# Three-tap convolutions on one Trainium2 core: six products per pair of tiles rewritten as five, with the even and odd positions kept apart

## The reference, cut to what matters

```python
CONVS = [(128, 10, 5)] + [(128, 3, 2)] * 4 + [(128, 2, 2)] * 2   # channels, taps, stride
h = x[:, None, :]
for w, g, b, s in zip(conv_ws, ln_gs, ln_bs, strides):
    h = _conv1d(h, w, s)                       # (64, 128, positions)
    h = jnp.swapaxes(h, -2, -1)
    h = _fp32_layernorm(h, g, b)               # over the 128 channels
    h = jnp.swapaxes(h, -2, -1)
    h = jax.nn.gelu(h, approximate=False)
```

## Time and profile before

| | us |
|---|---|
| median of three runs | 940.12 (937.58 to 946.72) |
| the profiled execution, its own time | 938.5 |
| its span, first to last instruction | 936.8 |
| of it: before the convolutions start | 54.9 |
| convolutions | about 490 |
| attention and experts | about 392 |

### The profile page before, as it was taken

How to read it: one execution, slowest core, us unless ns; L and a number is a source line. 1 busy time by engine, 2 the same in 40 slices (tenths; PEclk the granted TensorE clock), 3 DMA queues, 4 the chain that set the end, 5 groups by cost and what they waited for, 6 DMA issues and landing times. The chain is left out here.

```text
span 936.8 us, 12529 instructions
## 1 busy us (share of the span) xinstructions
PE 781.2 (83%) x4371; PEld 585.0 (62%) x4371; DVE 603.2 (64%) x1445; ACT 306.8 (33%) x506; POOL 215.7 (23%) x253
## 2 busy tenths in 40 slices
PE   0059998899979998899989758876888888799987
PEld 0026564556546565466655457866888887689977
DVE  4918655785648746324554556899788889654377
ACT  0043434433442334423422211402223331146433
POOL 3000000000000000000000003655688769148301
PEclk9999998899969899799989669989899999999999
DMA  1350330016000240000000034000000000200000
GB/s 57 44 128 1 63 81 1 0 23 121 1 1 0 33 98 0 0 1 1 1 1 1 0 129 184 1 1 1 1 0 0 0 0 0 75 2 1 1 0 26
DMA packets 22556, 25.34 MB, mean 27 GB/s; under 512 B 17052, under 2 KB 21212, under 8 KB 21404
## 3 DMA queue, kind: packets, MB, share of 16 engines
q1 hardware_dynamic: 22508, 24.74, 10.8%
HBM read 21.05 MB, written 3.66 MB: 26 GB/s over the span
## 5 line engine op out<-in xcount | busy, mean ns | idle before, releaser
L564 PE MATMUL ps<-h,w 128*128 128x400 f32 x720 | 290.9, 548 | 1.8 <-ACT h L632 1.7
L564 PEld LDWEIGHTS ps<-h,w 128*128 128x128 f32 x720 | 139.5, 200 | 106.0 <-issue 103.1
L724 DVE COPY h<-ps 128x800 f32<-128x800 f32 (+2 forms) x58 | 56.6, 975 | 94.4 <-PE ps L564 93.6
L577 PEld LDWEIGHTS ps<-averager,sq 128*100 128x100 f32 (+2 forms) x1024 | 99.3, 171 | 23.0 <-ACT sq L625 19.3
L577 PE MATMUL ps<-averager,sq 128*100 128x1 f32 (+2 forms) x1024 | 99.7, 227 | 8.9 <-ACT sq L625 8.4
L625 ACT ACTIVATE sq<-h 128x800 f32<-128x800 f32 (+2 forms) x58 | 49.8, 858 | 174.2 <-DVE h L724 174.2
L1075 PE MATMUL pt<-for_pe,ident 128*128 128x156 f32 (+2 forms) x420 | 69.9, 328 | 26.5 <-DVE for_pe L1274 26.5
L632 ACT ACTIVATE h<-h,lnp 128x800 f32<-128x800 f32 (+2 forms) x58 | 60.5, 1042 | 86.1 <-DVE h L755 84.4
L755 DVE TENSOR_TENSOR h<-h,ps 128x400 f32<-128x400 f32 (+2 forms) x116 | 60.0, 559 | 39.0 <-PE ps L593 38.9
L604 ACT ACTIVATE h<-ps,lnp 128x800 f32<-128x800 f32 x64 | 63.4, 1011 | 64.0 <-PE ps L525 63.8
L1112 POOL MEMSET eye<- 128x169 f32 x1 | 0.2, 240 | 360.7 <-PE pt L860 360.7
(11 more groups left out here) (272 smaller groups left out, 1156.7 us busy)
## 6 DMA issues: line engine op xcount, KB each, us to landing
late<-windows_dram SPq DMA_DIRECT2D x24, 375.0 KB, 7.5
gate_w<-in_gate_w SPq DMA_DIRECT2D x1, 3456.0 KB, 12.0
up_w<-in_up_w SPq DMA_DIRECT2D x1, 3456.0 KB, 18.7
windows_dram<-parts SPq DMA_DIRECT2D x12, 250.0 KB, 5.2
acts<-in_down_w SPq DMA_DIRECT2D x1, 1728.0 KB, 8.0
w<-in_w SPq DMA_DIRECT2D x1, 1024.0 KB, 5.3
xs<-in_x SPq DMA_DIRECT2D x4, 252.5 KB, 4.2
out_tokens<-hidden SPq DMA_DIRECT2D x6, 96.0 KB, 1.6
```

The costliest lines, as they stand in the source:

```text
L564: mm = pe.matmul(out, w[:, L.first_tap + t, :], source(l, s, 2 * p + c, t), start=(t == 0), stop=(t == L.taps - 1))
L577: mm = pe.matmul(var_ps[0:L.w, at:at + 1], sq[:, n["var"] % 2, c, q * L.w:(q + 1) * L.w], averager[:, 0:1], start=True, stop=True)
L724: nc.vector.tensor_copy(joined(l, s, p, r).rearrange("p (c b) t -> p c b t", c=2), ypair[n["bank"]][:, :, 0:L.cols].rearrange("p c (b t) - ...
```

## The change

Layers 1 to 3 keep their activations as two planes, even and odd positions. Two neighbouring outputs of one signal, at 2j and 2j+1, read the inputs e[2j], o[2j], e[2j+1] and e[2j+1], o[2j+1], e[2j+2] (e even plane, o odd plane). Their first and last taps share e[2j+1]. With w0, w1, w2 the taps, S = (w0+w2)·e[2j+1] is made once, and the outputs are w1·o[2j] + w0·(e[2j]-e[2j+1]) + S and w1·o[2j+1] - w2·(e[2j+1]-e[2j+2]) + S. The two banks of a pair now hold the even and the odd outputs of both chunks' signals, so a "chunk" is a plane.

- PE: "half" is two w1 matmuls and one of S into a bank of its own (`shared_ps`); "conv" is two matmuls of differences. Both wait for the inputs of the whole pair, `inputs_of`.
- GpSimd makes the differences e[i]-e[i+1] of a pair, two operations of 400 columns, into a ring of two (`diff`), as soon as the inputs are there and the pair two before is done.
- ScalarE copies S from PSUM to SBUF (`shared`), at the place of "half" in its queue.
- VectorE's copy out of PSUM becomes an addition of `shared`; w0+w2 and -w2 are made once at the start.
- The sums of squares and the turned rows now share one PSUM bank, so PE's "var" waits for DVE's copy of the rows before (`rows_ready`).
- GpSimd's copy into phases becomes a step at the head of the plan.
- PE's layer-0 matmuls read the windows at a step of two.

```diff
+PAIRED = (1, 2, 3)
+RING = 2
+    if not last:
+        step("phases", 0, 0)()
     prep(0, 2)
     conv(1, 0, 0, first(9))
...
+        shared_ps = ps[:, 6, :]
+        var_ps = ps[:, 7, 256:512]
+        rows_ps = ps[:, 7, 0:256].bitcast(BF16)
+        h0 = sb("h0", [P, 2, GROUP, 2, ROW0 // 2])
...
+        def plane(l, slot, p, parity, cut):
+            n = 2 * LAYERS[l].per_chunk
+            return (h0, h1, h2)[l - 1][:, slot, n * p:n * p + n, parity, cut]
+        def diffs(l, at, cut):
+            return diff[:, at, :].rearrange("p (b t) -> p b t", t=LAYERS[l].pos)[:, :, cut]
+        def inputs_of(plan, r, o, l, s, p):
+            if l == 1:
+                return y_taken, batch_taken(plan, r, o, GROUP * s + 2 * p + 1)
+            done = gelus_before(plan, l - 1, s)
+            return gelu_done, o.gelu + done[min(2 * p + 1, max(done))] + 1
...
+                        if what == "phases":
+                            spread_phases(r + 1)
+                        elif what == "half" and l in PAIRED:
+                            pool.wait_ge(*inputs_of(plan, r, o, l, s, p))
...
+                            for half in range(2):
+                                rows = slice(half * n, half * n + n)
+                                pool.tensor_tensor(to[:, rows, :], here[:, rows, :], behind[:, rows, :], ALU.subtract).then_inc(diff_ready, 1)
...
-                                       win[:, b * POS0 + h * 400:b * POS0 + h * 400 + 400], start=True, stop=True)
+                                       win[:, b * POS0 + h:(b + 1) * POS0:2], start=True, stop=True)
...
+                        elif what == "half" and l in PAIRED:
+                            pe.wait_ge(*inputs_of(plan, r, o, l, s, p))
+                            out = in_banks(l, ypair[n["bank"]][:, :, 0:L.cols])
+                            for c in range(2):
+                                pe.matmul(out[:, c, :, :], w[:, L.first_tap + 1, :], plane(l, s, p, 1, slice(c, L.pos, 2)), start=True, stop=False)
+                            pairs = o.paired + n["paired"]
+                            if not (isinstance(pairs, int) and pairs < 1):
+                                pe.wait_ge(shared_taken, pairs)
+                            pe.matmul(shared_ps[:, 0:L.cols].rearrange("p (b t) -> p b t", t=L.pos // 2), w_sum[:, l - 1, :],
+                                      plane(l, s, p, 0, slice(1, L.pos, 2)), start=True, stop=True).then_inc(shared_ready, 1)
+                        elif what == "conv" and l in PAIRED:
+                            pe.wait_ge(diff_ready, (o.paired + n["paired"] + 1) * 2)
+                            out = in_banks(l, ypair[n["bank"]][:, :, 0:L.cols])
+                            for c in range(2):
+                                mm = pe.matmul(out[:, c, :, :], w[:, L.first_tap + 2 * c, :], diffs(l, n["paired"] % RING, slice(c, L.pos, 2)),
+                                               start=False, stop=True)
+                            mm.then_inc(y_ready, 1)
...
+                            turned = o.sets + n["rows"]
+                            if not (isinstance(turned, int) and turned < 1):
+                                pe.wait_ge(rows_ready, turned)
...
+                        elif what == "half" and l in PAIRED:
+                            act.wait_ge(shared_ready, o.paired + n["paired"] + 1)
+                            act.copy(shared[:, n["paired"] % RING, :], shared_ps[:, 0:L.cols]).then_inc(shared_taken, 1)
...
+                            if l in PAIRED:
+                                dve.wait_ge(shared_taken, o.paired + n["paired"] + 1)
+                                both = shared[:, n["paired"] % RING, :].rearrange("p (b t) -> p b t", t=L.pos // 2)
+                                nc.vector.tensor_tensor(to, src, both.unsqueeze(1).broadcast_to([P, 2, 2 * L.per_chunk, L.pos // 2]),
+                                                        ALU.add).then_inc(y_copied, 1)
```

More of the change, by code:

```diff
@@ L233, in counted @@
 def counted(order):
-    n = dict.fromkeys(("pair", "half", "conv", "var", "norm", "rows", "scale", "gelu", "first", "prep"), 0)
+    n = dict.fromkeys(("pair", "half", "conv", "var", "norm", "rows", "scale", "gelu", "first", "prep", "phases", "paired"), 0)
     out, bank, held = [], 0, None
@@ L255, in counted @@
         n["pair"] += what in ("conv", "first")
+        n["paired"] += what == "conv" and l in PAIRED
     assert bank == 0 or not n["prep"]
@@ L266, in __init__, with pair_of @@
         self.scale, self.gelu = per["scale"] * rounds, per["gelu"] * rounds
+        self.paired = per["paired"] * rounds
 def number_of(plan, what, layer, slot, p, kind):
     return next(n[kind] for a, b, c, d, n in plan if (a, b, c, d) == (what, layer, slot, p))
+def pair_of(plan, paired):
+    return next(n["pair"] for what, l, s, p, n in plan if what == "conv" and l in PAIRED and n["paired"] == paired)
 def gelus_before(plan, layer, slot):
@@ L503, in _, with run @@
                                        base=-32 * a, pattern=[[-1, 8], [0, P]], channel_multiplier=1).then_inc(s_const, 1)
-                with pool.Fori(1, ROUNDS) as r:
-                    spread_phases(r)
+                def run(plan, r, o):
+                    for what, l, s, p, n in plan:
+                        if what == "phases":
+                            spread_phases(r + 1)
+                        elif what == "half" and l in PAIRED:
+                            at, pos = n["paired"] % RING, LAYERS[l].pos
+                            pool.wait_ge(*inputs_of(plan, r, o, l, s, p))
+                            if n["paired"] >= RING:
+                                pool.wait_ge(y_ready, o.pair + pair_of(plan, n["paired"] - RING) + 1)
+                            elif not (isinstance(r, int) and r == 0):
+                                pool.wait_ge(y_ready, o.pair - per["pair"] + pair_of(body, n["paired"] + per["paired"] - RING) + 1)
+                            here, behind = (plane(l, s, p, 0, slice(a, a + pos)) for a in range(2))
+                            to, n = diffs(l, at, slice(0, pos)), LAYERS[l].per_chunk
+                            for half in range(2):
+                                rows = slice(half * n, half * n + n)
+                                pool.tensor_tensor(to[:, rows, :], here[:, rows, :], behind[:, rows, :], ALU.subtract).then_inc(diff_ready, 1)
+                for_rounds(pool, run)
             CONSTS = 14
@@ L715, in _ @@
                 steps.settle()
+                ends = [w[:, t:t + 3 * len(PAIRED):3, :] for t in (0, 2)]
+                steps.done(nc.vector.tensor_tensor(w_sum[:, :, :], *ends, ALU.add))
+                steps.settle()
+                steps.done(nc.vector.tensor_scalar(ends[1], ends[1], -1.0, None, ALU.mult))
+                steps.settle()
                 nc.vector.nop(nofuse=True).then_inc(weights_ready, 1)
@@ L755, in run @@
                             nc.vector.tensor_tensor(h, h, spread[n["scale"] % 2][:, 0:L.cols].rearrange(
[L756 removed]
+                                "p (b t) -> p b t", t=h.shape[2]), ALU.mult).then_inc(scaled, 1)
                 start = steps.n
```

81 lines of the change are left out of this document (38 added, 43 removed).

## The result

The changed kernel takes 1034.39 us, median of four runs (1030.7 to 1039.27), against 940.12, which is a median of four as well: a ratio of 1.097 with a 95% interval of 1.092 to 1.102. The forecast was 984 us with a range of 955 to 1012. The direction was right, the size was not: +94 us where +44 was forecast. The profiled execution has a span of 1031.7 us and a mean granted clock of 0.866 instead of 0.937.

The account below looks back on a forecast made before the run. PE's queue was taken as the bound. Rounds 0 to 2 at +12.7 us each (+38) and the last at +5.5 gave +44 on 938.5, 982.5; with 1.6 for the median, 984 us, range 955 to 1012.

Parts of the forecast that it names:

- What bounds the kernel: In the convolutions PE's queue sets the end: busy 450.1 of 490.1 us, its matmuls of layers 1 to 4 almost never waiting.
- the wider wait: Layers 2 and 3: four halves a round wait for a later GELU, 12.0 us together, net +7.7 us a round.
- GpSimd's differences are hidden from "conv": In every layer the differences start with the half and run about 2 us while half takes 2.1 us, adding no wait.
- Layer 0 at a step of two: Layer 0's matmuls reading at a step of two cost 0; upper bound a doubling, +32 us.
- rival 4: Layer 0's matmuls at a step of two run at half rate and eat 32 us: 1016 us, chance 0.04.
- Rival 2: The waits are absorbed by PE's later waits in the round, about -5 us in all: 935 us, chance 0.08.
- rival 3: PE stays the bound throughout, with all 45 us gained: 894 us, chance 0.03.
- Rival 1: DVE and GpSimd always take turns, each difference blocking DVE fully in layer 1 and layer 3's norm: +78, 1018 us, chance 0.09.
- the strong form: Expectation set for the layer 1 differences run: each blocks VectorE fully, 1.7 us a pair, +16 us, 956 us.
- the clock: Layer 2: one or two halves behind the waits at the lower clock; +3 us a round, +2 in the last.
- the row copy's: Rest of layer 1: var's wait for DVE's row copy against 1.4 us two pairs save; 0 net, up to +1.5 us.
- Layer 1 and VectorE: Layer 1: GpSimd's differences slow DVE, 0.95 us a pair; +2 us a round, between -3 and +7; last round -4.5.

Follow-up runs that it names:

- b_wide: Kernel before, with only the first half's GELU wait in layers 2 and 3 widened to pair 2p+1: 1017.52 us, ratio 1.081.
- b_varwait: Kernel before, with only the wait of var for VectorE's row copy added: 957.62 us, ratio 1.018.
- b_pool: Kernel before, with GpSimd making unused differences beside layer 1 and PE's second half waiting for them: 955.4 us, ratio 1.014.
- a_tiny: Changed kernel, with GpSimd's differences cut to 8 columns of each signal, all waits kept: 1006.57 us, ratio 1.070.
- a_fill: Changed kernel, with products nobody reads (3, 6, 3 and 2) in front of the four GELU waits of each round: 998.07 us, ratio 1.061.
- b_fill: Kernel before, with products of 256 columns that nobody reads in front of PE's waits for the norm: 946.95 us, ratio 1.006.

## Why the prediction was right and wrong

| term, us in all | forecast | measured |
|---|---|---|
| four wider waits a round, idle time | 12.0 x 4 = 48 | 48.3 in the trace (1.8 before) |
| the clock behind them | +11 | 22 (filler, kernel before), 36 (filler, changed kernel) |
| wait for the row copy | 0, at most +1.5 a round | 16.5, 4.1 a round |
| GpSimd beside VectorE | from -3 to +2, three times: 15 | 13 in layer 1, 28 in all, clock included |
| products saved, as far as they count | about -30 | -16, clock included |

The forecast's five terms make +44; the measured ones, 76 for the widened wait with its clock, 16.5, 28 and -16, make 104 for a change of 94. The 10 between are not assigned by the experiments: the product was priced by putting one in, not by taking one out, and the differences were cut, not removed.

The two windows of the whole stage part the same loss in another way, by idle time and clock instead of by cause: +92 us are +67 of idle time, of which 46.5 are the GELU waits, -39 for the products at their full 0.70 us, and what remains, about +64, for the clock. The clock took more than the products gave. Its own column bears the 64 out: 0.79 over 586.9 us instead of 0.91 over 494.5 is some 157 us more at the lower level, and PE, busy four fifths of that time at half the speed, loses about 63. Both are estimates from the rows.

*What bounds the kernel* and the idle time in *the wider wait* held: the step from the dates of four GELUs and four halves to the idle time was right to a few tenths of a microsecond each. That GpSimd's differences are hidden from "conv" held: no wait of L612 is in the list. ACT's copy, VectorE's addition and GpSimd's time were right. Layer 0 at a step of two: its 128 instructions are busy 39.7 us instead of 36.2, with part of them at the lower clock; two of them take 0.53 us at the full one instead of 0.50, so rival 4 falls. Rival 2 falls by b_wide, rival 3 by the same rows. Rival 1 has the price of layer 1 nearly right (+13 in b_pool where the strong form gave 16), but 5 us of it come with the clock, and it was not the largest part.

The step that failed first is *the clock*: "I expect one or two of the halves behind them at the lower level". The trace has all four halves of round 1 there, and sums and convs in front or behind as well, and over the stage the clock costs about 64 us where +11 was set. I had taken one stretch, rows 10, as the model; b_varwait shows the clock falling in round 1 behind a wait of 1.73 us, although not behind one of 1.64 us in round 0. Over the stage a new wait cost more than itself: 76 us for 44 of idle time in b_wide, 18.8 us for 5.5 in the profiled execution of b_varwait.

The second is *the row copy's* "0 net". I set the 1.4 us that two pairs save against it; yet VectorE holds the row copy behind preparation in rounds 0 to 2 (1.6 to 1.7 us each time), and most of the price is again clock. The third is the size of *Layer 1 and VectorE*, 15 in the forecast and 28 in a_tiny: the differences also meet the norm (the rows at 229 us), those of layers 2 and 3 were set at nothing, and the clock behind them was not counted. At an unchanged clock b_pool's 8 us are not far above what the forecast's price gives for layer 1.

The Trainium skill, SBUF — State Buffer, "Who interferes with whom", was weighed ahead as the rule by which the term would be nearer to +7 a round. The traces agree with it on which operations are met: those with two SBUF inputs stretch from 0.19 to 0.8 us, the addition with one input in PSUM keeps its 991 ns. In rows 8 its case is the subtraction with two inputs beside GpSimd's copy; the cast behind it has one. On the size, b_pool stands between the 3 to 6 us of half the contention and the 16 of all of it: 8 us at an unchanged clock, 13 with it.

## What to carry to other kernels

Before work is taken from the engine that bounds, ask for every step that now needs more at once when the last of it is made, and put that date beside the date at which the engine arrives: two timelines gave these waits to a few tenths. Then price each new wait on TensorE at more than its idle time, since products behind it may run at the lower clock; if it can't be moved, a filler in front of it may be cheaper than nothing, but has to be measured (36 us gained in a_fill, 6 us lost in b_fill). Afterwards compare busy time for the same instructions as well as idle time: that parts the clock from the waits. And an engine that looks free may not be: GpSimd's elementwise work cost 28 us here, through VectorE and the clock.

## What the runs showed of the hardware

- Behind a wait of 1.73 us in a stretch of small products, three f32 products ran at the lower clock (3.85 us instead of 2.28, b_varwait, round 1); behind the same wait of 1.64 us in round 0 they did not (2.29 us). Behind the four waits of 1.99 to 4.72 us in round 1 of the changed kernel the products always did.
- One wait added to the kernel before lengthened PE's busy time for the same 2150 instructions by 13.3 us and its idle time by 5.5 (b_varwait).
- Fourteen more products a round, in front of waits, made a kernel 36 us faster (a_fill), with a mean clock of 0.907 to 0.915 instead of 0.855 to 0.866.
- One GpSimd difference of 400 columns (861 ns) stretches the one VectorE operation with two SBUF inputs that it meets from 0.19 to 0.8 us; a VectorE addition of PSUM and SBUF is not stretched (991 ns, 52 times).
